# Two pieces of the q and k projection moved between small products in the attention turns of a vision-tower kernel

## The chip, the cores and the metric

The kernel runs on one core of a Trainium2 chip. The metric is the device time of one execution in microseconds. It is a single program that holds the whole network. The engines are TensorE (PE, matmuls; PEld is its weight load), VectorE (DVE), ScalarE (ACT), GpSimd (POOL) and SyncE (SP); each works through its own list of instructions in order and they wait for one another by semaphores.

## What is computed

A token stage, a Mamba block, a mixture of experts with top-4 routing, an attention block and a linear layer, each with a residual and a layer norm before it, over 32 sequences of 65 tokens with 512 features. The change is in the code of the last two:

```python
h = h + _L1_attn_ref(_layernorm(h), W_qkv, W_o)
h = h + _L1_ffn_ref(_layernorm(h), weight, bias)

# attention, 16 heads of 32 features
qkv = einsum('bld,ed->ble', x, W_qkv)
q, k = _apply_rope(q), _apply_rope(k)
att = where(causal, einsum('bhqd,bhkd->bhqk', q, k) * scale, -inf)
y = einsum('bhqk,bhkd->bhqd', softmax(att), v)
out = einsum('bld,ed->ble', y, W_o)
```

## The kernel before

The function combine_attention_and_linear adds the experts' results, and does attention and the linear layer, in eight turns. A turn g handles a group of four sequences, called images 0 to 3 (260 tokens), in features x tokens layout, with 512 features as four tiles of 128. Three groups are in work at once: turn g does the attention of group g, the q, k and v projection of group g + 1 (named q in the code), the linear layer of group g - 1, and the adding of expert results and the first layer norm of group g + 2. Everything is written out by hand: one list for each engine, the order of a turn stands in the functions named turn, and waits on semaphore counts keep it correct.

What the change and the prediction touch, with lines of the kernel before:

- q_k(q, m), called in TensorE's turn, is one eighth of the q and k projection: 4 matmuls in the program (8 records, since a 32-bit matmul is recorded as two), 128 x 260, into one of two PSUM banks pR0 and pR1. Q_BANK gives the bank: m = 0, 3, 4, 6 use pR0 and m = 1, 2, 5, 7 use pR1. All projections are recorded under L1773: w_qk (q and k), w_f (linear), w_v (the v columns), w_o (output).
- take_qk(q, m) on ScalarE (L1987) copies a piece out of its bank into raw, and raises qk_ready.
- scores(g, b) on TensorE (L1818) makes the scores of image b, 32-row products; VectorE's open_scores (L2135, L2139, L2143) scales, masks and takes the maximum; GpSimd's subtract (L1677) and ScalarE's exps (L2004) follow; VectorE's close_scores (L2149, L2151, L2153) divides by the sum, and raises p_ready.
- values(g, b) on TensorE transposes the 16 heads' probabilities in three batches of 6, 5 and 5 (L1845) into two banks pT, and multiplies with v (L1854, 32 output rows each). ScalarE's take_image copies each batch (L2014) and then the result (L2020). The third batch must wait until the first is copied; in the timeline it stands as a row of its own, x5.
- mean(1, g-1), deviations (L2103), square (L1974), GpSimd's add_squares, var(1, g-1) (L1768, 2 records), ScalarE's root (L1978 Ln and L1980 Exp, each with a table load ahead of it) and normalize (L2108) are the layer norm of the group before. linear(g-1) (L1773 with w_f) needs it, and result (L2160) takes its tiles out of pR0 and pR1 in turn.
- turn_sum (L1746) transposes summed expert rows into a bank of pR, two or three times a turn; turns 6 and 7 have none.

On TensorE a turn before the change goes: scores 1, turn_sum 0, q_k 0 and 1, mean, q_k 2 and 3, values 0, scores 2, var, turn_sum 1, values 1, (turn_sum 2,) linear, scores 3, q_k 4 to 7, values 2, v columns, values 3, transposes of v, scores 0 of the next group, output projection. Turn 0 has no layer norm or linear of a group before; turn 7 has no q, k and v projection.

Of the kernel before, what the change touches and what calls it, by code (L numbers as in the profile page):

```python
# [24 lines left out]
FT = D // P  # L25
# [1534 lines left out]
def combine_attention_and_linear(nc, hT, ident, mean_w, weight, slot, y_d, tw, out_d):  # L1560
# [20 lines left out]
    with ExitStack() as ctx:  # L1581
# [3 lines left out]
        def sem(name):  # L1585
# [35 lines left out]
        qk_done, qk_ready, vt_done, vt_ready, v_done, v_ready, rot_steps, sin_ready, rope_ready = map(  # L1621
            sem, ("qk_done", "qk_ready", "vt_done", "vt_ready", "v_done", "v_ready", "rot_steps", "sin_ready", "rope_ready"))
# [9 lines left out]
        def place(c):  # L1632

            batch = next(b for b in map(batch_of, range(NG)) if c in b)
            return batch.index(c)
# [105 lines left out]
        def _(pe):  # L1741
            def turn_sum(c, bank):

                pe.wait_ge(taken, c * TOPK + TOPK)
                for k in range(FT):
                    mm = pe.transpose(pR[bank][:, k * TT:(k + 1) * TT], acc[place(c)][:, k * P:(k + 1) * P], ident[0:TT, 0:TT])  # L1746
                mm.then_inc(turned, 1)
# [28 lines left out]
            def linear(g, banks_free):  # L1776

                pe.wait_ge(ln_ready[1], g + 1)
                for m in range(FT):
                    if m < 2:  # L1780
                        banks_free(m)
                    else:
                        pe.wait_ge(out_ready, g * FT + m - 1)
                    project(m % 2, w_f, m, xl[1], f_done)

            def q_k(q, m):
                project(Q_BANK[m], w_qk, m, xl[0], qk_done)
# [46 lines left out]
            def values(g, b):  # L1834
                n = g * GB + b
                if b == 0:
                    pe.wait_ge(v_ready, g * GB + GB)
                pe.wait_ge(p_ready, n + 1)
                for u, unit in enumerate(UNITS):
                    nth = n * NU + u  # L1840
                    if nth >= 2:

                        pe.wait_ge(pt_ready, nth - 1)
                    for i, at in enumerate(unit):
                        mm = pe.transpose(pT[0:TOK, nth % 2, i * TOK:(i + 1) * TOK], S[b % 2][:, at, :], ident[0:TOK, 0:TOK])  # L1845
                    mm.then_inc(pt_done, 1)
                if n:
                    pe.wait_ge(y_ready, n)
                for u, unit in enumerate(UNITS):
                    pe.wait_ge(pt_ready, n * NU + u + 1)  # L1850
                    for at in unit:
                        i, r = ORDER[at]
                        h = i * HQ + r
                        mm = pe.matmul(pY[r * DH:(r + 1) * DH, i * TOK:(i + 1) * TOK], v[b][:, h * DH:(h + 1) * DH],  # L1854
                                       PT[u][:, at - unit[0], :], start=True, stop=True)
                mm.then_inc(y_done, 1)

            def turn(g, first=False, last=False):
                batch = batch_of(g + 2)
                q = g + 1  # L1860
                scores(g, 1)
                if batch:
                    if first:
                        pe.wait_ge(added, batch[0])
                    else:
                        pe.wait_ge(h_ready, g * FT)
                    turn_sum(batch[0], SUM_BANK[0])
                if not last:
                    pe.wait_ge(ln_ready[0], q + 1)
                    q_k(q, 0)  # L1870
                    if batch:
                        pe.wait_ge(added, batch[0] + 1)
                    else:
                        pe.wait_ge(h_ready, g * FT)
                    q_k(q, 1)
                    pe.wait_ge(qk_ready, q * 2 * FT + 1)
                if not first:
                    mean(1, g - 1)
                if not last:
                    pe.wait_ge(qk_ready, q * 2 * FT + 2)  # L1880
                    q_k(q, 2)
                    if not first:
                        pe.wait_ge(dev_ready[1], g)
                    q_k(q, 3)
                values(g, 0)
                scores(g, 2)
                if not last:
                    pe.wait_ge(qk_ready, q * 2 * FT + 4)
                if not first:
                    var(1, g - 1)  # L1890
                if batch:
                    turn_sum(batch[1], SUM_BANK[1])
                values(g, 1)
                if len(batch) > 2:
                    if not first:
                        pe.wait_ge(sd_ready[1], g)
                    turn_sum(batch[2], SUM_BANK[2])

                def sums_added(m):
                    if batch:  # L1900
                        pe.wait_ge(added, batch[min(1 + m, len(batch) - 1)] + 1)

                if not first:
                    linear(g - 1, sums_added)
                scores(g, 3)
                if not last:
                    if first:
                        pe.wait_ge(added, batch[-1] + 1)
                    for m in range(4, 2 * FT):
                        if m >= 6:  # L1910
                            pe.wait_ge(qk_ready, q * 2 * FT + m - 1)
                        elif not first:
                            pe.wait_ge(out_ready, (g - 1) * FT + m - 1)
                        q_k(q, m)
                values(g, 2)
                if not last:
                    v_columns(q)
                values(g, 3)
                if batch:
                    pe.wait_ge(vt_ready, q * FT + 3)  # L1920
                    mean(0, g + 2)
                if not last:
                    values_of(q)
                    scores(q, 0)
                pe.wait_ge(y_ready, g * GB + GB)
                if last:
                    pe.wait_ge(out_ready, g * FT)
                project(O_BANK[0], w_o, 0, yT, o_done)
                if batch:
                    pe.wait_ge(dev_ready[0], g + 3)  # L1930
                project(O_BANK[1], w_o, 1, yT, o_done)
                pe.wait_ge(h_ready, g * FT + 1)
                project(O_BANK[2], w_o, 2, yT, o_done)
                if batch:
                    pe.wait_ge(h_ready, g * FT + 2)
                    var(0, g + 2)
                pe.wait_ge(h_ready, g * FT + 3)
                project(O_BANK[3], w_o, 3, yT, o_done)
# [30 lines left out]
        def _(act):  # L1969
            act.wait_ge(eps_set, 1)  # L1970

            def square(n, q):
                act.wait_ge(dev_ready[n], q + 1)
                act.activation(sq[n][:, :, :], xl[n][:, :, :], ACT.Square).then_inc(sq_ready[n], 1)  # L1974
# [7 lines left out]
            def take_qk(q, m):  # L1982
                if m == 0 and q:

                    act.wait_ge(rope_ready, 2 * q)
                act.wait_ge(qk_done, q * 2 * FT + m + 1)
                act.activation(raw[:, m, :], pR[Q_BANK[m]][:, 0:GT], ACT.Copy).then_inc(qk_ready, 1)  # L1987
# [35 lines left out]
            def turn(g, first=False, last=False):  # L2023
                q = g + 1
                if not last:
                    take_qk(q, 0)
                    take_qk(q, 1)
                exps(g, 1)
                if not last:
                    take_qk(q, 2)  # L2030
                if not first:
                    square(1, g - 1)
                if not last:
                    take_qk(q, 3)
                take_image(g, 0)
                if not first:
                    root(1, g - 1)
                take_image(g, 1)
                exps(g, 2)
                if not last:  # L2040
                    take_qk(q, 4)
                    take_qk(q, 5)
                exps(g, 3)
                if not last:
                    take_qk(q, 6)
                    take_qk(q, 7)
                take_image(g, 2)
                if not last:
                    take_columns(q)
                take_image(g, 3)  # L2050
                if not last:
                    take_v(q)
                if batch_of(g + 2):
                    square(0, g + 2)
                if not last:
                    exps(q, 0)
                if batch_of(g + 2):
                    root(0, g + 2)
# [308 lines left out]
```

## Time and profile before

| | us |
|---|---|
| median of 3 runs | 2889.0 (2888.26 to 2889.16) |
| the profiled execution | 2887.97, span 2886.2 |
| busy in the span: PE / DVE / ACT / POOL | 2453.4 / 1936.5 / 1405.4 / 1215.9 |
| PE of the q, k projection (L1773, w_qk), 512 records | 126.7, 406 ns each |

The changed code runs from about 2327.8 us to the end of the span at 2886.2. A timeline row gives start, length, engine, line, operation, what is written from what, the count of merged instructions, and in brackets the engine's idle time ahead of it with what ended it. Where rows of an engine overlap by some tens of ns, ends are modelled.

### The profile page before, as it was taken

How to read it: one execution, taken by the hardware profiler on the slowest of the kernel's cores; microseconds unless marked ns; L12 is line 12 of the kernel's file. 1: busy time of each engine (PE TensorE's matmuls, PEld its weight loads, DVE VectorE, ACT ScalarE, POOL GpSimd, SP SyncE). 2: the span in 40 equal slices, each digit the busy share in tenths (PEclk: the TensorE clock that was granted, in tenths of full speed). 3: DMA queues.
4: the chain of work that ended last, by engine and by line, in shares of the span. 5: the costliest groups of instructions: out<-in, count | busy, mean ns of one | idle time of the engine just before them, and what ended most of it. 6: DMA issues, size and time to landing. Idle time of an engine off the chain costs nothing. (4 is left out here: it accounts for less than half of the span.)

```text
span 2886.2 us, 48591 instructions
## 1 busy us (share of the span) xinstructions
PE 2453.4 (85%) x17080; PEld 2089.8 (72%) x17081; DVE 1936.5 (67%) x2921; ACT 1405.4 (49%) x3474; POOL 1215.9 (42%) x774
## 2 busy tenths in 40 slices
PE   4999997788888888888887782999999579999986
PEld 4999997688887888888887771444444367877775
DVE  7665532999999999999999783222222366777562
ACT  0341335888888888888888430111111123343432
POOL 3200001666666666666666574000000365455331
PEclk9997987999999999999999955999999778999986
DMA  5910000000000000000000073556653221111000
GB/s 191 413 57 1 1 1 30 31 31 32 31 32 31 32 31 32 31 32 31 31 31 31 13 222 107 176 176 238 193 175 124 70 60 44 32 44 32 8 8 16
DMA packets 65440, 209.57 MB, mean 73 GB/s; under 512 B 12224, under 2 KB 17600, under 8 KB 62400
## 3 DMA queue, kind: packets, MB, share of 16 engines
q1 hardware_dynamic: 24832, 95.96, 9.6%
q0 software_dynamic: 28576, 89.16, 9.5%
q10 hardware_dynamic: 11808, 21.50, 2.0%
q8 instruction: 135, 2.21, 0.3%
q14 instruction: 89, 0.73, 0.1%
HBM read 129.96 MB, written 76.62 MB: 72 GB/s over the span
## 5 line engine op out<-in xcount | busy, mean ns | idle before, releaser
L846 POOL TENSOR_TENSOR m_hs<-m_hs,m_BC 128x1040 f32<-128x1040 f32 x256 | 619.0, 2418 | 382.6 <-DVE m_hs L959 382.6
L765 ACT ACTIVATE m_dA<-m_dt,m_A 128x128 f32<-128x128 f32 x2048 | 614.4, 393 | 185.9 <-DVE m_hs L959 111.4
L640 PE MATMUL m_py<-m_hs,ident 128*128 128x130 f32 x4096 | 534.9, 286 | 143.8 <-POOL m_hs L846 143.8
L640 PEld LDWEIGHTS m_py<-m_hs,ident 128*128 128x128 f32 x4096 | 501.8, 199 | 163.4 <-POOL m_hs L846 161.5
L959 DVE TENSOR_TENSOR_SCAN m_hs<-m_dA,m_own 128x1040 f32<-128x1040 f32 x256 | 593.2, 2317 | 35.5 <-ACT m_dA L765 22.7
L944 DVE TENSOR_TENSOR m_own<-m_BC,m_own 128x1040 f32<-128x1040 f32 x256 | 318.7, 1245 | 18.8 <-issue 4.9
L592 PE MATMUL m_pw<-m_xg,m_w_in 128*128 128x130 f32 x2048 | 268.0, 291 | 51.3 <-DVE m_xc L907 34.8
L592 PEld LDWEIGHTS m_pw<-m_xg,m_w_in 128*128 128x128 f32 x2048 | 259.2, 206 | 55.0 <-DVE m_xc L907 37.8
L1444 PE MATMUL e_pG<-ew_gu,e_xT 128*128 x656 | 236.2, 504 | 11.0 <-issue 7.4
L1424 POOL DMA_DIRECT2D e_x<-regions x80 | 42.9, 536 | 404.9 <-PE e_pX L1435 404.9
L1444 PEld LDWEIGHTS e_pG<-ew_gu,e_xT 128*128 128x128 f32 x656 | 120.0, 193 | 91.9 <-issue 26.1
L1515 DVE TENSOR_TENSOR e_h<-e_g,e_pG 128x192 f32<-128x192 f32 x82 | 29.1, 355 | 230.9 <-ACT e_g L1486 230.9
L1486 ACT ACTIVATE e_g<-e_pG 128x192 f32<-128x192 f32 x82 | 27.1, 330 | 225.4 <-PE e_pG L1444 225.4
L1773 PE MATMUL t_pR<-t_xl,tw_w_qk 128*128 128x260 f32 x512 | 126.7, 406 | 11.0 <-DVE t_xl L2108 9.1
L1492 ACT ACTIVATE e_y<-e_pY 128x512 f32<-128x512 f32 x82 | 49.0, 597 | 169.7 <-PE e_pY L1459 169.7
L811 POOL MEMSET m_pick<- 33x128 f32 x1 | 0.2, 198 | 298.9 <-POOLq L419 298.9
L1773 PEld LDWEIGHTS t_pR<-t_xl,tw_w_qk 128*128 128x128 f32 x512 | 100.9, 201 | 33.3 <-DVE t_xl L2108 11.4
L622 PE MATMUL m_pw<-m_y,m_w_out 128*128 128x130 f32 x1024 | 119.8, 275 | 0.4 <-DVE m_y L926 0.4
L622 PEld LDWEIGHTS m_pw<-m_y,m_w_out 128*128 128x128 f32 x1024 | 117.0, 190 | 0.6 <-DVE m_y L926 0.6
L153 PE MATMUL a_bank<-a_N 128*128 128x128 f32 (+1 forms) x1024 | 115.8, 277 | 0.0
L153 PEld LDWEIGHTS a_bank<-a_N 128*128 128x128 f32 x1024 | 115.7, 194 | 0.0
L1677 POOL TENSOR_TENSOR t_S<-t_S,t_top 65x1040 f32<-65x1040 f32 x32 | 66.3, 2073 | 106.8 <-DVE t_top L2143 106.7
(290 smaller groups left out, 4453.9 us busy)
## 6 DMA issues: line engine op xcount, KB each, us to landing
m_BC<-xs SPq DMA_DIRECT2D x16, 2080.0 KB, 9.9
slots<-a_zero POOLq DMA_DIRECT2D x48, 512.0 KB, 44.9
ew_gu<-in_gate_up_w SPq DMA_DIRECT2D x32, 768.0 KB, 5.0
e_x<-regions POOLq DMA_DIRECT2D x82, 256.0 KB, 3.0
slots<-e_y ACTq DMA_DIRECT2D x82, 256.0 KB, 2.6
regions<-a_zero POOLq DMA_DIRECT2D x16, 512.0 KB, 15.6
ew_d<-in_down_w SPq DMA_DIRECT2D x32, 256.0 KB, 5.6
out_h<-t_ho SPq DMA_DIRECT2D x8, 520.0 KB, 3.3
```

Of the source, the lines that this page charges most:

```text
L153: mm = pe.matmul(out(u)[:, h % NH, 0:HN if last else P], N[:, h, HN:3 * HN], N[:, h, 0:HN if last else 2 * HN], start=True, stop=True)
L592: mm = pe.matmul(pw[j][:, at * MT:(at + 1) * MT], w_in[:, k, (side * ET + e) * P:(side * ET + e + 1) * P], xg[b][:, k, :], start=(k == 0), ...
L622: mm = pe.matmul(pw[2 - 2 * part][:, at * MT:(at + 1) * MT], w_out[:, k, m * P:(m + 1) * P], y[b][:, k, :], start=(k == 0), stop=(k == ET ...
L640: mm = pe.matmul(py[k % 2][:, 0:MT], ident[:, :], hs[u % NB][:, n, :], start=False, stop=(half == 1 and n == HN - 1))
L765: act.activation(images(dA[u % NB][:, n, :])[:, :, 1:TOK], images(dt[b][:, k, :])[:, :, 1:TOK], ACT.Exp, scale=A[:, at:at + 1]).then_inc(d ...
L846: pool.tensor_tensor(hs[u % NB][:, :, :], hs[u % NB][:, :, :], BC[b][:, ST + half * HN:ST + (half + 1) * HN, :], ALU.mult).then_inc(prod_r ...
L944: dve.tensor_tensor(bu.rearrange("p (n t) -> p n t", t=MT), BC[b][:, half * HN:(half + 1) * HN, :], du[k % 3].unsqueeze(1).broadcast_to([P ...
L959: dve.tensor_tensor_scan(hs[u % NB][:, :, :].rearrange("p n t -> p (n t)"), dA[u % NB][:, :, :].rearrange("p n t -> p (n t)"), bu, 0.0, AL ...
L1444: mm = pe.matmul(pG[r][:, 0:2 * I], xT[r][:, k, :], w_gu[:, bass.ds(ring * FT + k, 1), :], start=(k == 0), stop=(k == FT - 1))
L1492: act.activation(y[r][:, :], pY[r][:, :], ACT.Copy).then_inc(y_ready, 1)
L1677: pool.tensor_tensor(S[b % 2][:, :, :], S[b % 2][:, :, :], top[b % 2][:, :].unsqueeze(2).broadcast_to([TOK, AH, TOK]), ALU.subtract).then_ ...
L1773: mm = pe.matmul(pR[bank][:, 0:GT], w[:, k, m * P:(m + 1) * P], x[:, k, :], start=(k == 0), stop=(k == FT - 1))
```

## The change

On TensorE, q_k 3 goes from ahead of values 0 to behind it, and q_k 4 from the group behind scores 3 to between scores 2 and var. So var, the layer norm of the group before, has both behind it. Since q_k 4 and turn_sum 1 share pR0, turn_sum 1 now waits until q_k 4 is copied (qk_ready); in turn 6, without turn_sum, the linear waits for this. The waits of q_k 5 to 7 are set anew to what holds their banks. On ScalarE, take_qk 3 goes behind take_image 0 and take_qk 4 right behind it, ahead of root. The loops run for turns 0 to 6.

```diff
@@ TensorE, turn @@
                     q_k(q, 2)
+                values(g, 0)
+                if not last:
                     if not first:
                         pe.wait_ge(dev_ready[1], g)
                     q_k(q, 3)
-                values(g, 0)
                 scores(g, 2)
                 if not last:
                     pe.wait_ge(qk_ready, q * 2 * FT + 4)
+                    q_k(q, 4)
                 if not first:
                     var(1, g - 1)
                 if batch:
+                    if not last:
+                        pe.wait_ge(qk_ready, q * 2 * FT + 5)
                     turn_sum(batch[1], SUM_BANK[1])
                 values(g, 1)
...
                 if not first:
+                    if not last and not batch:
+                        pe.wait_ge(qk_ready, q * 2 * FT + 5)
                     linear(g - 1, sums_added)
                 scores(g, 3)
...
-                    for m in range(4, 2 * FT):
-                        if m >= 6:
+                    for m in range(5, 2 * FT):
+                        if m == 7:
                             pe.wait_ge(qk_ready, q * 2 * FT + m - 1)
                         elif not first:
-                            pe.wait_ge(out_ready, (g - 1) * FT + m - 1)
+                            pe.wait_ge(out_ready, (g - 1) * FT + (4 if m == 5 else 3))
                         q_k(q, m)
@@ ScalarE, turn @@
+                take_image(g, 0)
                 if not last:
                     take_qk(q, 3)
-                take_image(g, 0)
+                    take_qk(q, 4)
                 if not first:
                     root(1, g - 1)
                 take_image(g, 1)
                 exps(g, 2)
                 if not last:
-                    take_qk(q, 4)
                     take_qk(q, 5)
```

TensorE in a turn with two turn_sums, from q_k 2 up to the v columns. A count here is of matmuls in the program, 4 for a piece q_k. Before:

```order
L1757 MATMUL t_pR<-t_hs,mean_w 128x260
L1773 MATMUL t_pR<-t_xl,tw_w_qk 128x260 x8
L1845 MATMUL t_pT<-ident,t_S 65x65 x16
L1854 MATMUL t_pY<-t_PT,t_v 32x65 x16
L1818 MATMUL t_pS<-t_qk 65x65 x16
L1768 MATMUL t_pR<-t_sq,mean_w 128x260
L1746 MATMUL t_pR<-ident,t_acc 128x104 x4
L1845 MATMUL t_pT<-ident,t_S 65x65 x16
L1854 MATMUL t_pY<-t_PT,t_v 32x65 x16
L1773 MATMUL t_pR<-t_xl,tw_w_f 128x260 x16
L1818 MATMUL t_pS<-t_qk 65x65 x16
L1773 MATMUL t_pR<-t_xl,tw_w_qk 128x260 x16
```

The same place after:

```order
L1757 MATMUL t_pR<-t_hs,mean_w 128x260
L1773 MATMUL t_pR<-t_xl,tw_w_qk 128x260 x4
L1845 MATMUL t_pT<-ident,t_S 65x65 x16
L1854 MATMUL t_pY<-t_PT,t_v 32x65 x16
L1773 MATMUL t_pR<-t_xl,tw_w_qk 128x260 x4
L1818 MATMUL t_pS<-t_qk 65x65 x16
L1773 MATMUL t_pR<-t_xl,tw_w_qk 128x260 x4
L1768 MATMUL t_pR<-t_sq,mean_w 128x260
L1746 MATMUL t_pR<-ident,t_acc 128x104 x4
L1845 MATMUL t_pT<-ident,t_S 65x65 x16
L1854 MATMUL t_pY<-t_PT,t_v 32x65 x16
L1773 MATMUL t_pR<-t_xl,tw_w_f 128x260 x16
```

A piece of 4 stands behind values 0 and another behind scores 2; the group behind scores 3 has 12 left instead of 16.

ScalarE from the copy of q_k 2 and the square of the layer norm up to exps 2. Before:

```order
L1974 ACTIVATE t_sq<-t_xl 128x1040
L1987 ACTIVATE t_raw<-t_pR 128x260
L2014 ACTIVATE t_PT<-t_pT 65x390
L2014 ACTIVATE t_PT<-t_pT 65x325 x2
L2020 ACTIVATE t_yT<-t_pY 128x4x65
L1978 ACT_TABLE_LOAD
L1978 ACTIVATE t_rstd<-t_pR,t_eps 128x260
L1980 ACT_TABLE_LOAD
L1980 ACTIVATE t_rstd<-t_rstd 128x260
L2014 ACTIVATE t_PT<-t_pT 65x390
```

After (line numbers are 6 higher):

```order
L1980 ACTIVATE t_sq<-t_xl 128x1040
L2020 ACTIVATE t_PT<-t_pT 65x390
L2020 ACTIVATE t_PT<-t_pT 65x325 x2
L2026 ACTIVATE t_yT<-t_pY 128x4x65
L1993 ACTIVATE t_raw<-t_pR 128x260 x2
L1984 ACT_TABLE_LOAD
L1984 ACTIVATE t_rstd<-t_pR,t_eps 128x260
L1986 ACT_TABLE_LOAD
L1986 ACTIVATE t_rstd<-t_rstd 128x260
L2020 ACTIVATE t_PT<-t_pT 65x390
```

The copies of pieces 3 and 4 stand between the copy of image 0's result and the first table load; before, that load followed the copy of the result directly.

## Rows read from the trace of the kernel before

**Rows 1.** The page, TensorE's granted clock in 40 slices of the span, in tenths.

```profile
PEclk9997987999999999999999955999999778999986
```

**Rows 2.** Windows, one for each turn (turns 0 and 5): length, busy us, PEclk, DMA.

```profile
2327.80:2402.10 74.30, 62.73 (x482) 52.79 (x481) 52.57 (x60) 22.28 (x43) 40.84 (x27) 0.79 0.19 54
...
2673.30:2738.50 65.20, 61.99 (x513) 52.21 (x512) 39.31 (x46) 26.05 (x47) 22.64 (x14) 0.92 0.03 9
```

**Rows 3.** Timeline of TensorE in turn 5, q_k 2 to values 2.

```profile
2680.58 3.77 PE L1773 MATMUL t_pR<-t_xl,tw_w_qk 128*128 128x260 f32 x16
2684.62 0.83 PE L1845 MATMUL t_pT<-ident,t_S 65*65 65x65 f32 x11 [0.26 <-issue]
...
2687.36 1.71 PE L1818 MATMUL t_pS<-t_qk 32*65 32x65 f32 x32
2689.00 0.89 PE L1768 MATMUL t_pR<-t_sq,mean_w 128*128 128x260 f32 x2
...
2692.57 0.81 PE L1845 MATMUL t_pT<-ident,t_S 65*65 65x65 f32 x5 [0.78 <-ACT t_PT L2014]
2693.31 1.98 PE L1854 MATMUL t_pY<-t_PT,t_v 65*32 65x65 f32 x32
2695.42 9.33 PE L1773 MATMUL t_pR<-t_xl,tw_w_f 128*128 128x260 f32 x32
...
2706.32 7.28 PE L1773 MATMUL t_pR<-t_xl,tw_w_qk 128*128 128x260 f32 x32
...
2714.54 0.51 PE L1845 MATMUL t_pT<-ident,t_S 65*65 65x65 f32 x5 [0.28 <-ACT t_PT L2014]
```

**Rows 4.** Timeline of ScalarE in turn 5, root and the end of exps 3.

```profile
2687.93 1.28 ACT L1978 ACT_TABLE_LOAD   x1
2689.93 0.48 ACT L1978 ACTIVATE t_rstd<-t_pR,t_eps 128x260 f32<-128x260 f32 x1 [0.71 <-PE t_pR L1768]
2690.42 1.28 ACT L1980 ACT_TABLE_LOAD   x1
2691.71 0.42 ACT L1980 ACTIVATE t_rstd<-t_rstd 128x260 f32<-128x260 f32 x1
2692.04 0.80 ACT L2014 ACTIVATE t_PT<-t_pT 65x390 f32<-65x390 f32 x2
...
2711.97 1.07 ACT L2004 ACTIVATE t_S<-t_S 65x1040 f32<-65x1040 f32 x1 [1.45 <-POOL t_S L1677]
...
2713.99 0.82 ACT L2014 ACTIVATE t_PT<-t_pT 65x390 f32<-65x390 f32 x2
```

**Rows 5.** Timelines of VectorE and GpSimd in turn 5.

```profile
2683.28 1.24 DVE L2153 TENSOR_TENSOR t_S<-t_S,t_den 65x1040 f32<-65x1040 f32 x1
...
2709.08 2.86 POOL L1677 TENSOR_TENSOR t_S<-t_S,t_top 65x1040 f32<-65x1040 f32 x1 [6.88 <-DVE t_top L2143]
```

**Rows 6.** Windows of turn 5, small products and linear.

```profile
2685.90:2689.30 3.40, 3.40 (x70) 3.17 (x70) 1.83 (x3) 2.23 (x4) 0.58 (x1) 1.00 0.02 5
2689.40:2692.80 3.40, 2.62 (x19) 2.24 (x18) 2.88 (x4) 2.85 (x5) 1.04 (x1) 0.50 0.00 0
...
2696.20:2699.60 3.40, 3.40 (x9) 2.63 (x9) 1.72 (x4) 0.47 (x1) 1.86 (x1) 0.50 0.00 0
2699.80:2703.20 3.40, 3.40 (x17) 2.96 (x16) 1.91 (x4) 0.00 (x0) 2.31 (x3) 1.00 0.00 0
```

**Rows 7.** Timelines of TensorE in turns 0, 1, 2, 3 and 4.

```profile
2374.95 0.51 PE L1845 MATMUL t_pT<-ident,t_S 65*65 65x65 f32 x5 [3.76 <-ACT t_PT L2014]
...
2416.14 2.70 PE L1818 MATMUL t_pS<-t_qk 32*65 32x65 f32 x32
...
2446.80 8.97 PE L1773 MATMUL t_pR<-t_xl,tw_w_v 128*128 128x260 f32 x32
...
2495.77 8.43 PE L1773 MATMUL t_pR<-t_xl,tw_w_f 128*128 128x260 f32 x32
...
2580.75 0.51 PE L1845 MATMUL t_pT<-ident,t_S 65*65 65x65 f32 x5 [2.08 <-ACT t_PT L2014]
...
2629.89 9.62 PE L1773 MATMUL t_pR<-t_xl,tw_w_f 128*128 128x260 f32 x32
```

## The prediction

> **What bounds the kernel now.** I read the page's slices first. The two changed lists (TensorE's and ScalarE's turn) run in the last fifth of the program, where TensorE's clock digit is mostly 9 with lower digits between [rows 1]. The windows by turn come next: there are eight turns, turn 0 lasts 74.3 us and turn 5, my example, 65.2 us, of which TensorE's matmuls are busy 62.0 [rows 2]. TensorE is the engine on which the turn is hung; what counts is what it waits for and at which clock it runs. The timeline of turn 5 on TensorE says so: the only holes are small ones behind ScalarE copies [rows 3]. The profiled execution took 2887.97 us (span 2886.2), 1.0 under the median of 2889.0. The sum is made against 2887.97, and 1.0 is added at the end.
>
> Three facts of turn 5 carry the argument. (1) In values(0) TensorE waits for the softmax of image 0: VectorE's last multiply ends at 2684.52 [rows 5], the first transpose starts at 2684.62. The piece q_k 3, the second half of the 3.77 us row at 2680.58, fills the time until 2684.35, so the wait is 0.26 us [rows 3]. (2) In values(1) the second batch of transposes (2692.57) waits for ScalarE's copy at 2692.04, and that copy stands behind root(1): a table load, Ln, a table load, Exp [rows 3, 4]. (3) The stretch from q_k 3 to the linear holds small products alone. The clock is 1.00 up to 2689.3 and 0.50, the 1.2 GHz level, from about 2689.4; at 2696.2 to 2699.6 it is still 0.50, with TensorE fully busy on the linear, and by 2699.8 it is 1.00 again, 2.4 GHz [rows 6]. The 32 matmuls of the linear take 9.33 us there where 32 of the same shape take 7.28 [rows 3]. The six linears of turns 1 to 6 take from 8.43 to 9.62 us [rows 7], a mean of about 9.1, so this costs 1.8 us in a turn.
>
> **The change, step by step** (turns 1 to 6; turn 7 projects nothing).
>
> A, q_k 3 goes behind values(0). It is 1.85 us (half of 3.77). Nothing that values(0) waits for comes earlier: mean(1), the deviations and both softmax closings keep their places. So TensorE idles 2.1 us where it idled 0.26, and pays the 1.85 behind. It costs 1.8 us a turn, all of it on the path; the scores of image 2 start 1.8 later. ScalarE's copy of q_k 3 goes behind take_image(0), where ScalarE waits anyway: nothing. 6 x 1.8 = 10.9.
>
> B, q_k 4 goes between the scores of image 2 and var(1). It is 1.8 us of matmuls, and var, root, normalize and the ScalarE copies of values(1) stand behind it. There is more: before, ScalarE's first table load ran at 2687.93, ahead of Ln's wait, while TensorE still did scores [rows 4]; now take_qk 4 precedes it. From the end of q_k 4 ScalarE needs 0.4 (copy), 1.28 (load), 0.48, 1.28, 0.42, and 0.53 passes from its copy's start to the second transposes (2692.04 to 2692.57): 4.4 us. Before, scores end at 2689.0 and the second transposes start at 2692.57: 3.57. Now it is 1.8 + 4.4 = 6.2. That is 2.7 in turn 5; where the clock had fallen earlier, about 2.4 (turn 1's scores lasted 2.70 instead of 1.71, [rows 7]). I take 2.5: 6 x 2.5 = 15.3. The new wait ahead of turn_sum 1 (qk_ready 5) costs nothing: var's 0.6 covers the 0.4 copy; behind it would be queued the transposes, which wait for root in any case. Without that cover it is 0.4 a turn at most. The bounds of B are 1.8 (a load that hides after all) and 2.7.
>
> C, what is given back behind the scores of image 3. There q_k 4 is missing, so values(2) could come 1.8 us sooner. But its second transposes wait for ScalarE's copy, which stands behind exps(3), and that behind GpSimd's subtract of 2.86 us from 2709.08 [rows 4, 5]. The exp ends at 2713.04; two copies of 0.36 must follow, so take_image starts at about 2713.65 instead of 2713.99. It gives back 0.35 of 1.8: 6 x 0.35 = -2.0.
>
> D, slack. In turns 1 and 3 three gathers are queued in GpSimd and values(2) waits longer already (2.08 us in turn 3, [rows 7]; about 0.5 over the common wait in turn 1). The shift of A and B before that place is hidden so far: -2.4 for both.
>
> E, the clock. A removes the dense piece ahead of values(0): 2.1 us of idling plus 2.8 of small products, a stretch of 4.9 us without a projection. B leaves var, turn_sum 1 and values(1), some 6 us of small work with over 2 us of idling, right ahead of the linear. The kernel before shows what such stretches do: the 3.4 us from 2685.9, of small products alone, ended with the clock down [rows 6], and the scores of the next image then ran at half speed in turn 1. I expect the clock to be low at the linear in 5 of 6 turns as before (saving 3.0 x 1/6 = 0.5 a turn: 1.8 of the linear, 0.3 and 0.7 of the small products at half speed, 0.2 of turn_sum). Of the stretches without a projection, those of 10 to 12 us ahead of the linear brought a fall in all six turns, and those of 2.7 us at values(2) in one of six (turn 1); 4.9 us lie between, and I take an estimate of 3 in 4 for a new fall in A's stretch, where q_k 3 itself then runs at half speed for most of its length (+1.9 x 3/4 = 1.4), less 0.4 that slowed scores cost before. And values(2), now 4.4 us from projection to projection, lets the clock fall in front of the v columns more often than once in six (8.97 us in turn 1 [rows 7] against 7.28, so 1.7 each time): +0.4. Together +0.9 a turn, 5 in all. The bounds are -3.4 a turn (never low) and +6.
>
> F, turn 0. q_k 3 goes behind values(0), where ScalarE is held up anyway, at a half clock (up to 3.7 us), and q_k 4 behind the scores. Against that, turn 0's values(2) already waited 3.76 us for ScalarE [rows 7], so the removal behind gives nothing. The whole chain after it hangs on the scores of image 2. Bounds -3.5 (clock up through the turn) to +7; I take +3.5.
>
> Sum: 10.9 + 15.3 - 2.0 - 2.4 + 5 + 3.5 = 30.3. 2887.97 + 30.3 + 1.0 = **2919 us**, 1.0% slower.
>
> A rule on the clock stands apart. The Trainium skill ("TensorE: Matmul & The Clock Gate", What's actually happening) holds that the reduced clock is the default and that activity releases it. Taken alone, this speaks for two projection pieces among the small products and would give rival 1. The same page (Part 4: PE-mode transpose) says that transposes don't count as busy in the same way. The rows at 2685.9 and 2689.4, where TensorE is full with small products and the clock falls, agree with the second. The sum needs neither.
>
> **Rivals.**
> 1. The clock stays up. The two pieces break 12 us of small products into shorter stretches; if that is enough, the linear takes 7.28 and nothing is slow. Worked out for turn 5: scores of image 2 start at 2687.36 + 1.84 = 2689.2 and end at 2690.85; q_k 4 ends at 2692.7; second transposes at 2697.1; linear from 2699.0 to 2706.3, 1.6 later than now; less 0.35, +1.25. By the same working turns 1 and 4 come out at about -0.3 and -0.1, turns 2, 3 and 6 at 1.1 to 1.5: +4.7 in all. With D's -2.4, turn 0's -3.5 and the two chance falls of 1.7 each that turns 1 and 2 show now, it is -4.6: 2884 us, not slower. It decides if 4.9 us without a projection, then 6 us, keep the clock at 1.00. Against it: in turn 5 the clock was down 5 us after the end of q_k 3, with only small products between [rows 3, 6].
> 2. The waits are not TensorE's. If GpSimd or VectorE set each turn as they do in part of turns 1 and 3, A and B vanish and only C's clock effects stay: 2887 to 2893. For it, the 2.08 us; against it, in turns 2, 4, 5 and 6 TensorE waits 0.3 us there.
> 3. The clock falls in A's stretch and does not come back before the linear: q_k 3, scores and q_k 4 at half speed, +1.8, +1.1, +1.8, and a fall at every v columns, +1.7. Less what E already counts, some 5 a turn: 2919 + 30 = 2949.
>
> **How the numbers follow.** The forecast case has a chance of 0.73, rival 1 0.13, rival 2 0.08, rival 3 0.06. A difference under 0.2% (5.8 us) can't be told from no change. Rival 1 gives faster 0.06 and same 0.07 (more chance falls can go or stay), rival 2 same 0.04, faster 0.01 and slower 0.03, the rest is slower: faster 0.07, same 0.11, slower 0.82. The range leaves out rival 1 and rival 3: its low end is the forecast with E at -3 a turn and F at zero (2893), its high end has E at some +4.5 (2940).
>
> **What would show it.** A: in each of turns 1 to 6 an idle time of about 2.1 us before the first transposes of values(0), with the softmax multiply as releaser. B: the table load of root(1) starts behind take_qk 4, and the second transposes of values(1) wait about 2.5 us for ScalarE. C: a hole of about 1.6 us in values(2) instead of 0.3. E: the linear still at 8.4 to 9.7 us, and some rows of q_k 3 at 2.5 us or more. Turns 1 to 6 grow by 3 to 7 us each, turn 7 doesn't change. The prediction is wrong if the linears take 7.3 us, or if the hole in front of values(0) doesn't appear.

## The result and the profile after

The changed kernel takes 2937.1 us (median; 2927.4 to 2940.1), the kernel before 2888.6 beside it. The ratio is 1.0167, interval 1.0155 to 1.0180: 48.5 us slower, 1.7%. The forecast was 2919, 30 us slower. The sign and the three waits are right; the size of the clock's term is not. (The profiled execution took 2940.1 us, 52.1 over the profiled one of the kernel before.)

The page of the kernel after, TensorE's granted clock in 40 slices (it answers to [rows 1]), shows more lowered digits in the last quarter:

```profile
PEclk9998977999999999999999757999998778888887
```

Windows of the kernel after, one for each turn (length, then busy us of PE, PEld, DVE, ACT, POOL, clock, DMA share, GB/s), turns 0 to 7, to be read against [rows 2]:

```profile
2328.70:2407.70 79.00, 65.82 (x482) 54.03 (x481) 50.54 (x60) 22.42 (x43) 40.83 (x27) 0.74 0.18 51
2407.70:2484.10 76.40, 67.65 (x514) 55.73 (x513) 48.27 (x58) 25.50 (x46) 36.80 (x26) 0.87 0.15 41
...
2707.30:2782.20 74.90, 66.94 (x513) 54.98 (x512) 37.93 (x46) 25.83 (x47) 22.66 (x14) 0.86 0.02 8
...
2856.70:2938.40 81.70, 52.88 (x393) 43.15 (x392) 29.97 (x38) 18.65 (x29) 14.73 (x11) 0.71 0.04 14
```

The loss is in the changed turns. Turn 0 grew by 4.7 us, turns 1 to 6 by 7.6, 5.6, 6.9, 8.4, 9.7 and 9.9, 48 us together, and turn 7, which has no projection, became 1.3 us shorter. In turn 5 the matmuls are busy 66.94 us where they were 61.99, with the same 513 records and no work added: 5 us of that turn's 9.7 are the same matmuls running longer. The clock's mean fell from 0.92 to 0.86.

TensorE's timeline of turn 5 after, against [rows 3]:

```profile
2710.37 5.46 PE L1773 MATMUL t_pR<-t_xl,tw_w_qk 128*128 128x260 f32 x16 [0.83 <-DVE t_xl L2114]
2716.31 2.02 PE L1773 MATMUL t_pR<-t_xl,tw_w_qk 128*128 128x260 f32 x8
2720.35 0.89 PE L1845 MATMUL t_pT<-ident,t_S 65*65 65x65 f32 x11 [2.02 <-issue]
...
2722.21 1.98 PE L1854 MATMUL t_pY<-t_PT,t_v 65*32 65x65 f32 x32
2724.13 3.83 PE L1773 MATMUL t_pR<-t_xl,tw_w_qk 128*128 128x260 f32 x8
2727.89 1.71 PE L1818 MATMUL t_pS<-t_qk 32*65 32x65 f32 x32
2729.53 2.02 PE L1773 MATMUL t_pR<-t_xl,tw_w_qk 128*128 128x260 f32 x8
...
2735.93 0.81 PE L1845 MATMUL t_pT<-ident,t_S 65*65 65x65 f32 x5 [2.67 <-ACT t_PT L2020]
...
2738.58 8.69 PE L1773 MATMUL t_pR<-t_xl,tw_w_f 128*128 128x260 f32 x32
...
2748.84 5.53 PE L1773 MATMUL t_pR<-t_xl,tw_w_qk 128*128 128x260 f32 x24
2756.54 0.51 PE L1845 MATMUL t_pT<-ident,t_S 65*65 65x65 f32 x5 [1.52 <-ACT t_PT L2020]
...
2758.16 8.97 PE L1773 MATMUL t_pR<-t_xl,tw_w_v 128*128 128x260 f32 x32
```

Three holes stand where the prediction put them: 2.02 us ahead of values 0, 2.67 in values 1, 1.52 in values 2. The first is the wait for the softmax: the row names only "issue", but VectorE's multiply (L2159) starts at 2719.01 and takes 1.24, so it ends 0.1 ahead of the transposes. And the matmuls beside them are long: q_k 3, 8 records, takes 3.83 us where q_k 4 takes 2.02; q_k 0 and 1 take 5.46 instead of 3.77; the v columns 8.97 instead of 7.28. The windows of the same turn give the clock there:

```profile
2711.00:2714.00 3.00, 3.00 (x8) 2.35 (x7) 2.26 (x3) 0.03 (x1) 0.62 (x1) 0.50 0.00 0
2717.70:2720.90 3.20, 1.18 (x12) 0.78 (x12) 3.13 (x4) 1.35 (x2) 1.10 (x1) 1.00 0.00 0
2721.10:2727.50 6.40, 6.17 (x47) 4.89 (x45) 2.14 (x3) 1.48 (x4) 1.03 (x2) 0.50 0.01 3
2728.20:2734.50 6.30, 5.01 (x56) 4.16 (x53) 2.53 (x3) 3.05 (x5) 1.93 (x1) 1.00 0.00 0
2735.00:2741.00 6.00, 5.07 (x43) 4.31 (x44) 4.13 (x5) 2.97 (x7) 1.27 (x1) 0.50 0.01 3
...
2759.00:2761.80 2.80, 2.80 (x8) 2.18 (x7) 1.76 (x3) 0.04 (x1) 0.96 (x1) 0.50 0.00 0
2762.20:2780.00 17.80, 17.27 (x147) 14.68 (x145) 5.99 (x8) 6.96 (x13) 4.97 (x4) 1.00 0.01 1
```

This turn had one fall of the clock in the kernel before [rows 6]; now it has four: in q_k 0, in the stretch with the new hole, ahead of the linear, and at the v columns. Three of the four come in or right behind a hole that the change made or widened. Counted in this way, turns 1 to 6 have 21 falls after and 8 before.

Not every stretch of small products brings a fall. The one from values 3 to the output projection (transposes, 32-row products, the transposes of v, scores) ends at full clock:

```profile
2766.97 0.81 PE L1845 MATMUL t_pT<-ident,t_S 65*65 65x65 f32 x11
...
2774.22 5.53 PE L1773 MATMUL t_pR<-t_yT,tw_w_o 128*128 128x260 f32 x24
```

That is 7.2 us, with a clock of 1.00 through it (the last window above). The output projection's 24 records run as fast as those of q_k 5 to 7 (5.53). The output projection starts at full clock in every one of turns 1 to 6, before and after.

ScalarE's timeline of turn 5 after, against [rows 4], shows why the second hole is as long as it is:

```profile
2731.59 0.39 ACT L1993 ACTIVATE t_raw<-t_pR 128x260 f32<-128x260 f32 x1 [3.21 <-PE t_pR L1773]
2731.99 1.28 ACT L1984 ACT_TABLE_LOAD   x1
2733.28 0.48 ACT L1984 ACTIVATE t_rstd<-t_pR,t_eps 128x260 f32<-128x260 f32 x1
2733.78 1.28 ACT L1986 ACT_TABLE_LOAD   x1
```

The table load now begins only when the copy of q_k 4 is done, and Ln follows it with no wait of its own. Before, the load had run earlier and Ln waited 0.71 us for TensorE [rows 4].

### The profile page after: what moved, and what is told of

The parts are those of the page before. It is cut to its first block and busy times, and to the rows that moved or that the text cites. A ratio compares the mean times of both kernels' runs of the same rounds, so it can differ in the third digit from the quotient of the medians.

```text
span 2938.4 us, 48591 instructions
## 1 busy us (share of the span) xinstructions
PE 2476.6 (84%) x17080; PEld 2101.0 (72%) x17081; DVE 1925.9 (66%) x2921; ACT 1405.5 (48%) x3474; POOL 1214.3 (41%) x774
## 5 line engine op out<-in xcount | busy, mean ns | idle before, releaser
L1773 PE MATMUL t_pR<-t_xl,tw_w_qk 128*128 128x260 f32 x512 | 151.3, 457 | 11.0 <-DVE t_xl L2114 9.1
L1773 PEld LDWEIGHTS t_pR<-t_xl,tw_w_qk 128*128 128x128 f32 x512 | 112.8, 227 | 39.4 <-DVE t_xl L2114 11.4
L1993 ACT ACTIVATE t_raw<-t_pR 128x260 f32<-128x260 f32 x64 | 23.8, 383 | 193.1 <-PE t_pR L1773 193.1
```

What stands on the lines that cost most here:

```text
L1773: mm = pe.matmul(pR[bank][:, 0:GT], w[:, k, m * P:(m + 1) * P], x[:, k, :], start=(k == 0), stop=(k == FT - 1))
```

## The experiments

Ratios are to the kernel before on the same chip, since the kernel before itself takes 2888.5, 2908.2 and 2884.7 us on the three chips used here. The code ahead of turn 0 is the same in all kernels, but its length differs between executions: turn 0 starts at 2327.8 us in the kernel before and at 2319.9 to 2323.5 in the profiled executions of the next four. So where profiles are compared, turns are compared by themselves.

### One part at a time

The first kernel keeps q_k 3 behind values 0 and puts q_k 4 back:

```diff
                     q_k(q, 2)
-                    if not first:
-                        pe.wait_ge(dev_ready[1], g)
-                    q_k(q, 3)
                 values(g, 0)
+                if not last:
+                    if not first:
+                        pe.wait_ge(dev_ready[1], g)
+                    q_k(q, 3)
```

> Only piece q_k 3 stands behind values 0; q_k 4 is back behind the scores of image 3, and so are their copies on ScalarE. Theory (uncovered wait, and a clock that falls in more places): 1.8 us for each of turns 1 to 6 from the wait, some 3 for turn 0, and up to 3 a turn from the clock, since q_k 3 then runs at half speed and the stretch up to the linear is as long as before: 2910 to 2920, with a hole of 2.0 us ahead of values 0 in turns 1 to 6. Rival (order alone, the clock does not matter): 2888.6 + 14 = 2902. Rival (A is hidden and B makes all of the loss): 2889 to 2892.

Measured: 2917.3 us, ratio 1.0099 (1.0084 to 1.0113), 29 us slower. That is within what the theory gave and twice what order alone gave. Its TensorE timeline in turn 4, from q_k 0 to the linear:

```profile
2615.74 5.46 PE L1773 MATMUL t_pR<-t_xl,tw_w_qk 128*128 128x260 f32 x16 [0.83 <-DVE t_xl L2109]
...
2625.72 0.83 PE L1845 MATMUL t_pT<-ident,t_S 65*65 65x65 f32 x11 [2.02 <-issue]
...
2629.49 3.84 PE L1773 MATMUL t_pR<-t_xl,tw_w_qk 128*128 128x260 f32 x8
...
2641.44 10.09 PE L1773 MATMUL t_pR<-t_xl,tw_w_f 128*128 128x260 f32 x32 [0.75 <-DVE hT L2097]
```

The hole is 2.02 us and q_k 3 takes 3.84, where a row of the same 8 records at full clock takes 2.02: the wait is 1.8 us more than before and the half clock at q_k 3 alone another 1.8. One more cost came that the expectation did not name: the linear now waits for VectorE's addition of the expert sums (0.75 to 1.35 us in turns 1 to 5) and then takes 9.8 to 10.1 us, where the kernel before has 8.4 to 9.6.

The second keeps q_k 4 between the scores and the variance and puts q_k 3 back ahead of values 0:

```diff
                 scores(g, 2)
                 if not last:
                     pe.wait_ge(qk_ready, q * 2 * FT + 4)
+                    q_k(q, 4)
                 if not first:
                     var(1, g - 1)
```

> Only piece q_k 4 stands between the scores of image 2 and the variance; q_k 3 is ahead of values 0 as in the kernel before. Theory: 2.4 to 2.7 us a turn at the second transposes of values 1, 0.35 given back behind the scores of image 3, less the slack of turns 1 and 3, about +11 from order alone, and 1.7 a turn where the v columns now begin at half speed behind a hole of 1.5 us in values 2, about +10: 2905 to 2915. Rival (the piece keeps the clock up and the linear takes 7.3 us): 2885 to 2895.

Measured: 2912.1 us, ratio 1.0086 (1.0072 to 1.0099), 24 us slower, inside the theory's range and far from the rival's. Its turns 4 and 5:

```profile
2658.69 0.51 PE L1845 MATMUL t_pT<-ident,t_S 65*65 65x65 f32 x5 [1.52 <-ACT t_PT L2020]
...
2660.31 8.97 PE L1773 MATMUL t_pR<-t_xl,tw_w_v 128*128 128x260 f32 x32
...
2701.76 3.71 PE L1773 MATMUL t_pR<-t_xl,tw_w_qk 128*128 128x260 f32 x8
...
2712.51 8.77 PE L1773 MATMUL t_pR<-t_xl,tw_w_f 128*128 128x260 f32 x32
```

The linear still takes 8.77 (8.50 to 9.12 in turns 1 to 6): the piece between the small products does not keep the clock up. It is itself caught at half speed in turns 2 to 6 (3.67 to 3.83), a cost that the theory did not name. The two parts alone cost 29 and 24 us by the medians, 53 against 48.5 together. In turns 1 to 6 of the profiled executions they cost 35.7 and 27.6, 63 against 48. So they overlap in part: in the changed kernel the linear comes later, does not wait for VectorE and takes 8.4 to 9.7 us.

### The table load

```diff
                 take_image(g, 0)
+                if not first:
+                    act.activation(scratch[:, :], eps[:, 0:1], ACT.Ln)
                 if not last:
                     take_qk(q, 3)
                     take_qk(q, 4)
```

> The changed kernel with a Ln of one column on ScalarE behind the copies of image 0's result, ahead of the copies of pieces 3 and 4, so that the table load runs while TensorE does q_k 3. Theory (B's term holds 1.3 us a turn of a table load that is no longer hidden): the idle time ahead of the second transposes of values 1 falls from 2.7 to about 1.4 us in turns 1 to 6, 8 us in all, about 2929; the clock's falls may shift and give or take 5. Rival (the load is hidden, the wait is for Ln's own input): the idle time stays at 2.7 and the time within 1 us of the changed kernel's, 2937.

Measured: 2924.1 us, ratio 1.0128 (1.0113 to 1.0144), 13 us less than the changed kernel's. Its turn 5:

```profile
2721.39 0.51 PE L1846 MATMUL t_pT<-ident,t_S 65*65 65x65 f32 x5 [1.41 <-ACT t_PT L2021]
...
2723.01 7.28 PE L1774 MATMUL t_pR<-t_xl,tw_w_f 128*128 128x260 f32 x32
```

The wait fell from 2.67 to 1.41, by 1.26 in the turn, which is the 1.28 of a load: this part of B is shown. It fell by as much in turns 2 to 6 and by 0.75 in turn 1, 7 us in all. The other 6 us have a candidate in the second row: with the shorter hole the linear ran at full speed in this turn and in two others (7.28 to 7.37). In the other three it took 8.86 to 9.43, behind the same wait or a longer one, so the shorter hole alone does not decide it. The next run tests holes and clock more directly.

### Filling the holes with useless matmuls

```diff
+            def fill(n):
+                for _ in range(n):
+                    pe.matmul(pY[:, 0:GT], mean_w[:, :], xl[0][:, 0, :], start=True, stop=True)
+
             def values(g, b):
                 n = g * GB + b
+                if b == 0 and 0 < g < NG - 1:
+                    fill(4)
                 if b == 0:
                     pe.wait_ge(v_ready, g * GB + GB)
...
+                    if u == 2 and 0 < g < NG - 1 and b in (1, 2):
+                        pe.wait_ge(y_ready, n)
+                        fill(4 if b == 1 else 3)
                     if nth >= 2:
                         pe.wait_ge(pt_ready, nth - 1)
```

> The changed kernel with extra 128x128x260 matmuls on TensorE whose results are overwritten (4 in the hole ahead of values 0, 4 in the hole of values 1, 3 in the hole of values 2, turns 1 to 6), sized to 1.85, 1.85 and 1.4 us so that they fit into the idle times of 2.0, 2.7 and 1.5. They do no needed work. Theory (some 5 us a turn of the loss are TensorE at half clock, brought on by the holes): linear 7.3 to 8, v columns 7.3, q_k 3 1.9 to 2.0, time 2900 to 2912. Rival (the loss is the waits alone): no gain, 2937 or more, as the holes are filled with useless work.

Measured: 2905.0 us, ratio 1.0060 (1.0046 to 1.0073), with the changed kernel at 1.0167: 32 us less from adding 66 matmuls that compute nothing. Its turn 5 on TensorE:

```profile
2692.85 1.92 PE L1836 MATMUL t_pY<-t_xl,mean_w 128*128 128x260 f32 x8
2695.03 0.83 PE L1854 MATMUL t_pT<-ident,t_S 65*65 65x65 f32 x11 [0.26 <-issue]
...
2697.77 2.02 PE L1773 MATMUL t_pR<-t_xl,tw_w_qk 128*128 128x260 f32 x8
...
2704.92 1.97 PE L1836 MATMUL t_pY<-t_xl,mean_w 128*128 128x260 f32 x8
2707.76 0.51 PE L1854 MATMUL t_pT<-ident,t_S 65*65 65x65 f32 x5 [0.87 <-ACT t_PT L2029]
...
2709.38 7.28 PE L1773 MATMUL t_pR<-t_xl,tw_w_f 128*128 128x260 f32 x32
...
2727.55 7.28 PE L1773 MATMUL t_pR<-t_xl,tw_w_v 128*128 128x260 f32 x32
```

The needed work and its order are as in the changed kernel; the first transposes still wait for the softmax, behind 1.92 us of filler instead of idle time. But q_k 3 takes 2.02 instead of 3.83, the linear and the v columns 7.28. Useless work in the holes can't bring anything it waits for earlier, so the 32 us were TensorE at half clock, and dense work in place of the idle time took them away. In turns 1 to 6 of the profiled executions it is 31.6 us. Not all of it belongs to the loss against the kernel before, whose own linears ran slow, and it is not all of the clock's share: the fall in q_k 0 and 1, where no filler stands, came in all six turns (5.43 in this one), the v columns stayed slow in turns 1 and 3 (8.97 and 8.86) and the linear in turn 6 (8.92). In turns 1 and 3, where GpSimd has three gathers, 2.3 us of the gain went into a longer wait in values 2.

### Can the kernel before be improved the same way?

The old order with fillers: 1 in the wait ahead of q_k 0, 2 between values 0 and the scores of image 2, 3 in the wait of values 1. The cut shows the 2; the others are calls of the same kind.

```diff
                 values(g, 0)
+                if not first and not last:
+                    fill(2, pT[:, 0, 0:GT])
                 scores(g, 2)
```

> The kernel before, in its old order, with useless 128x128x260 matmuls on TensorE in turns 1 to 6: 1 in the wait ahead of q_k 0, 2 between values 0 and the scores of image 2, 3 in the wait of values 1. Theory (the clock at the linear costs some 3 us a turn in the kernel before, too): the 2 between products cost 0.9 us a turn, the others nothing; linears fall to 7.3 to 7.6 us, the products of values 1 to 1.25, so 2 us a turn are left, 2874 to 2880. Rival (the clock's fall is hidden behind other engines' work): 2889 + 5 = 2894.

Measured: 2909.5 us on a chip where the kernel before takes 2908.2, ratio 1.0006 (0.9995 to 1.0017). No gain; the 9 to 15 us of the theory did not come, and the loss of 5 of its rival did not come either. It was run again beside a profile of the kernel before:

> The kernel before, unchanged, profiled once more beside the next two: on the chip of fill_before and early4 it takes 2908 us instead of 2889, and without a profile of it there the holes of those two can't be told from the chip's. If it is the chip, turns 1 and 3 (three gathers each) last about 72 us here as they do in fill_before, against 68.8 and 68.3; if the fillers made them longer, they last 68 to 69. On a chip like the first, it takes 2889.

> fill_before again beside a profile of the kernel before. Theory (fillers keep the clock up at a cost of 0.9 us a turn, and the gain of 2 us a turn stands wherever GpSimd's gathers do not bound the turn): 8 to 12 us faster than the kernel before on the first chip, in turns 2, 4, 5 and 6; nothing in turns 1 and 3, where values 2 waits for GpSimd. Rival (a filler ahead of the scores delays the whole chain behind it by as much as it saves): within 3 us of the kernel before on either chip.

Measured: the kernel before 2885.0 (1.0006), and with fillers 2883.6, ratio 0.9994 (0.9984 to 1.0004). That chip was a third one, where turns 1 and 3 of the kernel before last 70.1 and 68.8 us, so the question about the second chip is not answered by it. The kernel with fillers was profiled on both, and there 25 of 32 us lie ahead of turn 0 (it starts at 2345.6 and at 2320.8), in code that no kernel here changes; the cause stays open. The expectation of 8 to 12 us is refuted, and its rival's number, within 3 us, came. Turn 2, 67.3 us instead of 65.3, shows one way in which the gain was lost. With fillers:

```profile
2481.06 1.15 PE L1836 MATMUL t_pT<-tw_cos,mean_w 128*128 128x260 f32 x4
...
2490.20 7.25 PE L1773 MATMUL t_pR<-t_xl,tw_w_f 128*128 128x260 f32 x32 [0.85 <-DVE hT L2107]
...
2500.34 8.97 PE L1773 MATMUL t_pR<-t_xl,tw_w_qk 128*128 128x260 f32 x32 [1.24 <-DVE t_ho L2171]
```

The kernel before on the same chip, turn 2:

```profile
2487.95 8.04 PE L1773 MATMUL t_pR<-t_xl,tw_w_f 128*128 128x260 f32 x32
...
2497.56 7.28 PE L1773 MATMUL t_pR<-t_xl,tw_w_qk 128*128 128x260 f32 x32
```

The linear does run at full clock, 7.25 to 7.28 us in turns 1 to 6 (8.04 to 9.75 in the kernel before here). But it starts behind a wait of 0.85 for VectorE's addition of the expert sums (0.85 to 1.35 in turns 2 to 5), and q_k 4 waits 1.24 for a result that VectorE takes out of a bank: where TensorE was slow it hid VectorE, and now VectorE is late next. Behind that wait q_k 4 to 7 run slow (8.97 instead of 7.28). With the 1.1 us of the fillers between products, that is more than the linear and the small products gave here. The other turns differ: turns 3 to 5 became 0.3, 1.5 and 0.8 us shorter, while in turns 1 and 6 (2.0 and 1.6 longer) the clock fell among the fillers and the scores of image 2 (2.84 and 2.83 instead of 1.71), so there the fall had moved and not gone.

Needed work as the filler: q_k 4 between values 0 and the scores, its copy behind those of image 0, and the first two of ScalarE's three copies of image 2 ahead of exps 3 (take_image now makes the call that it is given ahead of its third copy).

```diff
                 values(g, 0)
+                if not last:
+                    pe.wait_ge(qk_ready, q * 2 * FT + 4)
+                    q_k(q, 4)
                 scores(g, 2)
...
                 if not last:
-                    take_qk(q, 4)
                     take_qk(q, 5)
-                exps(g, 3)
-                if not last:
                     take_qk(q, 6)
                     take_qk(q, 7)
-                take_image(g, 2)
+                take_image(g, 2, lambda: exps(g, 3))
```

> Needed work as the filler, from the kernel before: q_k 3 stays ahead of values 0, q_k 4 goes between values 0 and the scores of image 2, its copy behind take_image 0; and on ScalarE the copies of q_k 5 to 7 and the first two copies of image 2 go ahead of exps 3, the third behind it. Theory: no new hole ahead of values 0, the table load stays hidden, the 1.8 us of q_k 4 are given back behind the scores of image 3 since values 2 no longer waits for exps 3; the linear may still begin at half clock. 2880 to 2890. Rival (the give-back fails, as in term C): +1.5 us a turn, 2898.

Measured: 2921.4 us, ratio 1.0046 (1.0032 to 1.0059), on the second chip, 13 us slower than the kernel before there. Theory (1 slower to 9 faster) and rival (9 slower) both failed. Its turn 4 has no new hole ahead of values 0 and has the give-back (0.29 ahead of the second transposes of values 2, which were 1.52 in the changed kernel), but values 1 has a hole of 3.08 us, the linear takes 8.58 us and q_k 5 waits for VectorE:

```profile
2646.88 2.02 PE L1773 MATMUL t_pR<-t_xl,tw_w_qk 128*128 128x260 f32 x8
...
2655.26 0.81 PE L1845 MATMUL t_pT<-ident,t_S 65*65 65x65 f32 x5 [3.08 <-ACT t_PT L2021]
...
2658.66 8.58 PE L1773 MATMUL t_pR<-t_xl,tw_w_f 128*128 128x260 f32 x32
...
2669.68 5.53 PE L1773 MATMUL t_pR<-t_xl,tw_w_qk 128*128 128x260 f32 x24 [0.80 <-DVE t_ho L2166]
```

The hole in values 1 is 3.00 to 3.08 us in turns 1 to 4 and 1.67 and 2.03 in turns 5 and 6. The table load is hidden, as the theory has it, but Ln begins 2.00 us behind it, though TensorE's rows of var end earlier. On the third chip, in the next kernel, the same wait of Ln is 0.59. What held it no row shows.

With 1 and 3 useless matmuls in the two waits added:

> The same as early4 with 1 useless matmul in the wait ahead of q_k 0 and 3 in the wait of values 1, turns 1 to 6. Theory: the clock is at 1.00 through the linear in most turns, no filler is on the path, 3 us a turn less: 2865 to 2875. Rival (the stretch behind q_k 4 still lets the clock fall, or VectorE's results bound the linear): 2880 or more.

Measured: 2902.5 us, ratio 0.9982 (0.9970 to 0.9993) on the second chip, 6 us faster than the kernel before there. The theory gave 14 to 24; the rival is what came.

> early4_fill again beside a profile of the kernel before; needed work stands as the filler ahead of the scores. Theory: turns 2, 4, 5 and 6 shorter than before by 1 to 3 us each, turns 1 and 3 longer by some, since the later scores of image 2 delay GpSimd's gathers and exps 3: 4 to 10 us faster than the kernel before. Rival: the same as the kernel before within 3 us.

Measured on the third chip: 2886.3 us, ratio 1.0008 (0.9999 to 1.0017). The theory's 4 to 10 us did not come, the rival did. So it is no better than the kernel before in a way that holds from chip to chip. The two orders with fillers, run on two chips each, lie within 6 us of the kernel before, and none is handed on as an improvement.

## Why the prediction was right in sign and short in size

Each term is added up over turns 1 to 6 from the starts of the rows in both timelines.

**A, the uncovered wait (10.9 us).** Right: the hole is 2.01 to 2.02 us in all six turns, where 2.1 was written, against 0.26 before, and 11.2 us came.

**B, q_k 4 ahead of the variance (15.3 us).** Right: in turn 5 the scores end at 2729.5 and the second transposes start at 2735.9, 6.4 us, where 6.2 was written and 3.57 was before. Over the six turns 15.3 us came, q_k 4 counted at full clock. By turns it is 2.8 in turn 5, where 2.7 was written, and 2.5 in the others. The table load's part is shown by itself, 1.26 a turn of it. (6 x 2.5 is 15.0 and not 15.3, which changes nothing.)

**C, what is given back (0.35 a turn), and D, slack (2.4).** Right: in turn 5, from the start of the group behind scores 3 to the second transposes it is 7.7 us after and 8.2 before, so 0.5 came back of q_k 4's 1.8. The hole is 1.52, the text said about 1.6. In turns 1 and 3 another 0.5 and 1.8 us came back, 2.3 in all: this is D.

**F, turn 0 (3.5 us).** 4.7.

**E, the clock (5 us in all).** This term was mis-sized, and it is nearly the whole error. q_k 3 takes 3.59 to 3.84 us in all six turns, +11.2 against full clock; the products of values 0 beside it and their last transposes +6.0; the v columns take 8.97 in five turns instead of one, +6.7; q_k 0 and 1 take 5.46 in four turns instead of one, +5.0; q_k 4 in turn 1 +1.8; the scores of image 2 -0.8; the end of values 1, faster in turns 1 and 2, and what follows it up to the linear -1.8; the six linears, 8.37 to 9.72, -1.3 together. That is 27 us. The other growth of these turns, 48 less 27 or 21 us, is the order's share; A to D made it 21.8.

The step that failed is the one that set E by chances from the length of stretches without a projection: 3 in 4 for a fall in A's stretch, and "more often than once in six" at the v columns, priced at a quarter. In the profiled execution the falls came in six of six and in five of six turns. The same step left out the products of values 0, slowed with q_k 3, and q_k 0 and 1, which the change doesn't touch. The rows of the kernel before spoke against length as the measure: it had 7.2 us from values 3 to the output projection with no fall in any turn, and in turn 3 4.5 us at values 2 (from 2577.86 to 2582.36) with none either, where the prediction took 2.7 for all six. And the linear had been slow in all six turns before, not in 5 of 6. What does decide where a fall comes stays open. With E at 4.5 a turn the prediction had drawn the high end of its range, 2940, and that is what came (27 us in six turns): the median lies 3 us inside it.

Rival 1, the clock stays up, is refuted: q_k 3 is itself slowed in all six turns, q_k 4 in turn 1, and the linears still take 8.4 to 9.7 us. Rival 2, other engines hide it, is refuted by the 48 us. Rival 3's mechanism came in part: the clock did come back before the linear in turns 2 to 6 (q_k 4 takes 2.02) and only in turn 1 did not, but the falls at q_k 3 and at the v columns were those it named, and the time (2937) lies between the forecast and it. Turns 1 to 6 grew by 5.6 to 9.9 us, where 3 to 7 was written. The rule of the Trainium skill ("TensorE: Matmul & The Clock Gate", Part 4: PE-mode transpose) that transposes don't count as busy in the same way agrees with the trace only in part. The stretch ahead of the linear, with transposes in it, ends at 0.50 [rows 6], but the 7.2 us from values 3 to the output projection, with more transposes, stay at 1.00. The fillers show that dense work in place of the idle time keeps the clock up in the changed kernel; what transposes and 32-row products do apart no run here separates.

Executions of the changed kernel differ by 12.7 us (2927.4 to 2940.1), those of the kernel before by 5.3 in the same comparison. With some 20 falls of the clock in the changed turns, each worth 1.7 to 2 us, it is likely that some of them come in one execution and not in another; a second profile of the changed kernel, which would show it, was not taken.

## What to carry to other kernels

An idle stretch on TensorE can cost twice: the wait, and the half clock of the matmuls behind it (here the clock's part was 27 us, that of waits and order 21). Where work is moved away from in front of a wait, price the hole it leaves plus the slowed matmuls after it at every such place in the loop, also where the edit doesn't reach. As an upper bound take a fall in every turn: here it came in 4 to 6 of six at each place. And before moving an item ahead of a chain on another engine, look at what that engine did in the gap: here a table load of 1.28 us had been hidden in a wait.

## What the runs showed of the hardware that was not expected

Useless matmuls in idle time made the changed kernel 32 us faster (1.0167 to 1.0060), 66 of them in six turns. The same means in the kernel before took nothing off (0.9994 and 1.0006), though the linears went from 8.04 to 9.75 us down to 7.25: VectorE was late next, and in two turns the fall only moved. A stretch of 7.2 us of transposes, 32-row products and scores stayed at full clock in every turn, while shorter ones with a hole of 2.0 us in them did not (5.5 to 5.9 us from the end of q_k 2 to q_k 3, in six of six turns). The kernel before took 2888.5, 2908.2 and 2884.7 us on three chips; so only ratios on one chip were compared.
